# Two attention blocks on one core: phi's weight folded into theta's, z as keys, small jobs through one PSUM bank, loops unrolled

## The reference

```python
# block 1 (no softmax), 64 inner channels
g_x, theta_x, phi_x = W_g x + b_g, W_theta x + b_theta, W_phi x + b_phi
y = ((theta_x.T @ phi_x) / 1024) @ g_x.T
x = x + W_out y.T + b_out
# block 2, 128 channels; z is block 1's result
theta, phi = W_t z + b_t, W_p z + b_p
attn = softmax(theta.T @ phi / sqrt(128))
out = z + W_c (z attn.T) + b_c
```

## Time and profile before

| what | us |
|---|---|
| median of 3 runs | 178.74 |
| lowest, highest | 178.66, 178.77 |
| span of the profiled execution, first to last instruction | 176.7 |
| TensorE busy | 170.2 (96%) |
| VectorE busy | 131.4 (74%) |
| ScalarE busy | 103.1 (58%) |
| GpSimd busy | 35.8 (20%) |

### The profile page before, as it was taken

One profiled execution on the slowest core, in us unless ns is written; L12 is line 12 of the kernel. 1 busy time (PEld: TensorE's weight loads), 2 busy tenths in 40 slices (PEclk: granted clock), 3 DMA queues, 4 the chain that ended last, 5 costly groups with the idle time before them and its releaser, 6 DMA issues.

```text
span 176.7 us, 2720 instructions
## 1 busy us (share of the span) xinstructions
PE 170.2 (96%) x974; PEld 138.9 (79%) x974; DVE 131.4 (74%) x189; ACT 103.1 (58%) x176; POOL 35.8 (20%) x32
## 2 busy tenths in 40 slices
PE   7899998999999999999999999999999999998994
PEld 7784585788889887888889787988888888876794
DVE  0315889886987776896988676796989689899811
ACT  3024477858683365958684274958686557656410
POOL 1105600003102200543202200443302202340000
PEclk9999999999999999999999999999999999999999
DMA  4600000003001000013001000010000100100011
GB/s 137 190 0 0 4 0 0 0 4 118 1 2 59 2 4 0 0 59 91 32 0 57 3 0 0 0 59 0 0 0 18 41 4 0 59 2 0 0 63 59
DMA packets 2537, 4.71 MB, mean 27 GB/s; under 512 B 288, under 2 KB 992, under 8 KB 2528
## 3 DMA queue, kind: packets, MB, share of 16 engines
q1 hardware_dynamic: 2096, 4.26, 7.1%
q10 hardware_dynamic: 432, 0.33, 0.8%
HBM read 2.49 MB, written 2.10 MB: 26 GB/s over the span
## 4 chain that ended last, share of the span: by engine, by line
PE 83%; DVE 5%; ACT 5%; DMA 4%; SPq 1%; issue 1%; ACTq 0%; DVEq 0%
PE ring L254 29%; PE ring L334 21%; PE turned L304 14%; PE ring L262 4%; DMA X<-x_dram 4%; ACT P L567 3%; PE ring L244 3%; PE ring L317 3%; PE ring L208 2%; DVE negmax L695 2%; DVE PT_lo L710 2%; ACT PT_hi L576 2%; PE ring L219 2%; PE turned L208 1%; PE ring L495 1%; PE ring L288 1%
## 5 line engine op out<-in xcount | busy, mean ns | idle before, releaser
L576 ACT ACTIVATE PT_hi<-turned 128x512 fp32r<-128x512 f32 x62 | 35.9, 595 | 26.5 <-PE turned L304 26.5
L695 DVE TENSOR_REDUCE negmax<-ring 128x1 f32<-128x1024 f32 x32 | 39.1, 1222 | 15.3 <-PE ring L254 15.1
L567 ACT ACTIVATE P<-ring,negmax 128x1024 f32<-128x1024 f32 x32 | 35.8, 1118 | 19.0 <-DVE negmax L695 19.0
L710 DVE TENSOR_TENSOR PT_lo<-turned,PT_hi 128x512 fp32r<-128x512 f32 x62 | 42.1, 684 | 5.2 <-ACT PT_hi L576 4.7
L304 PE MATMUL turned<-identity,P 128*128 128x128 f32 x256 | 36.1, 274 | 2.1 <-DVE P L703 1.6
L304 PEld LDWEIGHTS turned<-identity,P 128*128 128x128 f32 x256 | 30.4, 141 | 9.0 <-DVE P L703 1.6
L703 DVE TENSOR_SCALAR P<-P,rden 128x1024 f32<-128x1024 f32 x32 | 27.0, 845 | 1.1
L334 PE MATMUL ring<-PT_hi,V_hi 128*128 128x512 f32 x56 | 23.5, 420 | 0.1
L334 PE MATMUL ring<-PT_lo,V_hi 128*128 128x512 f32 x56 | 22.2, 396 | 0.0
L334 PE MATMUL ring<-PT_hi,V_lo 128*128 128x512 f32 x56 | 22.1, 395 | 0.0
L254 PE MATMUL ring<-Phi_hi,T_hi 128*128 128x512 f32 x62 | 21.3, 424 | 0.0
(11 more groups left out here) (101 smaller groups left out, 200.3 us busy)
## 6 DMA issues: line engine op xcount, KB each, us to landing
out_dram<-result SPq DMA_DIRECT2D x7, 256.0 KB, 2.0
X<-x_dram SPq DMA_DIRECT2D x3, 512.0 KB, 3.3
X_first<-x_dram SPq DMA_DIRECT2D x2, 256.0 KB, 4.1
w<-weights_dram ACTq DMA_DIRECT2D x1, 194.0 KB, 5.8
out_dram<-result SPq DMA_DIRECT2D x1, 192.0 KB, 1.9
wi<-inner_dram SPq DMA_DIRECT2D x1, 64.2 KB, 5.9
pg_w<-pg_weights_dram ACTq DMA_DIRECT2D x1, 64.0 KB, 3.2
pg_b<-pg_bias_dram ACTq DMA_DIRECT2D x1, 64.0 KB, 5.5
```

Of the source, the lines that this page charges most:

```text
L567: nc.scalar.activation(P[:, t % P_BUFFERS, :], ring[:, slots[t], :], ACT.Exp, bias=negmax[:, t:t + 1], accum_out=den[:, t:t + 1]).then_inc ...
L576: nc.scalar.activation(PT_hi[:, g, half_chunks(h), k * TILE:(k + 1) * TILE], turned[:, columns(h)].rearrange("p (j r) -> p j r", j=CHUNKS_ ...
L695: nc.vector.tensor_reduce(negmax[:, t:t + 1], ring[:, slots[t], :], AX.X, ALU.max, negate=True).then_inc(max_ready, 1)
L710: nc.vector.tensor_tensor(PT_lo[:, g, half_chunks(h), rows], turned[:, columns(h)].rearrange("p (j r) -> p j r", j=CHUNKS_PER_HALF), PT_hi ...
```

## The change

What it does:

- **Scores from z.** `theta.T phi` is `(W_t z + b_t).T (W_p z + b_p)`. Once, at the start, U is made from both weights (two transposes, one 128-column product, three one-column products, scaled by 128^-0.5 in ScalarE's copy). Per image only `t = U z + u` is computed, and the keys are z itself, in its high and low part. The phi conv and its evacuation are gone. What phi's bias adds to a query's row of scores is constant over the row; it is carried as `rho`, two extra columns of the values' weight (`VW`, 130 columns), and added to the row's maximum: after `row_max` a new operation on 128x1, `shift`, waits for the maximum and gives the bias of the exp.
- **Padding.** M, R and the inner weights, 64 rows before, are 128 rows with zeros.
- **One bank for small jobs.** PSUM is now `ring` (two slots of two banks, scores only), `turned`, `numer` and one bank `aux`. All jobs for image b+1 go through `aux`, in the order pg0, pg1, MT, R, A, Z0, Z1, t0, V0, V1, V2, t1. Each waits until the one before has been evacuated (`aux_free`). pg, z and t are made in halves, the values in three parts.
- **Order.** No hardware loops. One sequence of 32 tiles, n = 0 to 31; in tile n: scores(n+2), half a turn, `job_one`, a piece of attend (from n = 4), half a turn, `job_two`. The values of image b+1 are made in image b.
- **First image.** x, z and t of image 0 go by three passes too; V in three parts between, with their evacuations.
- **Engines.** High parts of x and z of the later images are made by GpSimd instead of ScalarE. The residual operation is gone: the last bias is added in `copy_numer`, and `finish` adds z. x has two buffers, z three, t and V two.

The core of the diff, in the order of the new file:

```diff
-        w = sb("w", [C, W_COLS])
-        wi = sb("wi", [CI, I_COLS])
+        wi = sb("wi", [C, I_COLS])
+        w = sb("w", [C, 2 * C])
+        bias = sb("bias", [C, 4])
+        VW = sb("VW", [C, V_COLS])
+        U = sb("U", [C, C + 3])
+        UT_hi, UT_lo = sb("UT_hi", [C, C], F32R), sb("UT_lo", [C, C], F32R)
...
-        ring = ctx.enter_context(nc.psum_tensor("ring", [C, 3, PIX], F32))
-        numer, small = ring[:, 2, 0:BANK], ring[:, 2, BANK:PIX]
+        ring = ctx.enter_context(nc.psum_tensor("ring", [C, 2, PIX], F32))
+        numer = ctx.enter_context(nc.psum_tensor("numer", [C, BANK], F32))
+        aux = ctx.enter_context(nc.psum_tensor("aux", [C, BANK], F32))
...
+            def job_pg(b, half):
+                pe.wait_ge(aux_free, aux_before(b, f"pg{half}"))
+                if half == 0:
+                    pe.wait_ge(x_loaded[b], 16)
+                phi_g_chunks(b, aux, half).then_inc(aux_ready, 1)
...
+            def queries(b, bank, cols):
+                return three(bank, (UT_hi[:, :], UT_lo[:, :]), (Z_hi[:, b % 2, :], Z_lo[:, b % 2, :]), cols)
+            def job_t(b, half):
+                pe.wait_ge(aux_free, aux_before(b, f"t{half}"))
+                if b:
+                    pe.wait_ge(z_lo, (b - 1) * HALVES + half + 1)
+                queries(b, aux[:, :], columns(half)).then_inc(aux_ready, 1)
...
+            job_A(0)
+            pe.wait_ge(aux_free, aux_after(0, "A"))
+            for half in range(HALVES):
+                pe.wait_ge(first_x_lo, half + 1)
+                affine_half(ring[:, 1, columns(half)], half).then_inc(first_z, 1)
+            pe.wait_ge(u_lo, 1)
+            pe.wait_ge(first_z_lo, 1)
+            queries(0, first_t_bank(0), FIRST_T[0]).then_inc(first_t, 1)
+            pe.wait_ge(first_z_ready, 1)
...
+            value_chunks(0, numer, 0).then_inc(first_v, 1)
+            scores(0)
+            queries(0, first_t_bank(1), FIRST_T[1]).then_inc(first_t, 1)
+            job_t(0, 1)
+            pe.wait_ge(first_z_ready, 2)
+            scores(1)
+            for part in (1, 2):
+                pe.wait_ge(first_v_lo, part)
+                value_chunks(0, numer, part).then_inc(first_v, 1)
...
+            for n in range(ALL - 1):
+                b, t = divmod(n, TILES)
+                if n + 2 < ALL:
+                    scores(n + 2)
+                turn(n, 0)
+                if b + 1 < IMAGES:
+                    job_one(b + 1, t)
+                if n >= GT:
+                    attend(n // GT - 1, n % GT)
+                turn(n, 1)
+                if b + 1 < IMAGES:
+                    job_two(b + 1, t)
+            attend(ALL_GROUPS - 2, PIECES - 1)
...
+            first_z_copy(0)
+            act.wait_ge(u_copied, 1)
+            first_t_high(0)
+            first_z_copy(1)
+            first_v_high(0)
+            first_t_high(1)
+            high_t(0, 1)
+            exps(0)
+            exps(1)
+            first_v_high(1)
+            first_v_high(2)
...
+            for n in range(ALL - 1):
+                b, t = divmod(n, TILES)
+                high_turned(n, 0)
+                if b + 1 < IMAGES:
+                    job_one(b + 1, t)
+                if n + 2 < ALL:
+                    exps(n + 2)
+                high_turned(n, 1)
+                if n >= GT and n % GT == GT - 1:
+                    copy_numer(n // GT - 1)
+                if b + 1 < IMAGES:
+                    job_two(b + 1, t)
...
+                dve.wait_ge(max_ready, n + 1)
+                nc.vector.tensor_scalar(shift[:, t:t + 1], negmax[:, t:t + 1], rho[:, b % 2, t:t + 1],
+                                        rho[:, b % 2, t:t + 1], ALU.subtract, ALU.add).then_inc(shift_ready, 1)
...
+            first_z_low(0)
+            first_t_low(0)
+            first_z_low(1)
+            first_v_low(0)
+            first_t_low(1)
+            row_max(0)
+            low_t(0, 1)
+            row_max(1)
+            norm(0)
+            first_v_low(1)
+            first_v_low(2)
...
+            for n in range(ALL - 1):
+                b, t = divmod(n, TILES)
+                if n + 2 < ALL:
+                    row_max(n + 2)
+                low_turned(n, 0)
+                if b + 1 < IMAGES:
+                    job_one(b + 1, t)
+                norm(n + 1)
+                low_turned(n, 1)
+                if b + 1 < IMAGES:
+                    job_two(b + 1, t)
...
+            def split_z(b, half):
+                count = (b - 1) * HALVES + half + 1
+                cols = columns(half)
+                pool.wait_ge(aux_free, aux_after(b, f"Z{half}"))
+                nc.gpsimd.tensor_copy(Z_hi[:, b % 2, cols], Z[:, b % Z_BUFFERS, cols]).then_inc(z_hi, 1)
+                pool.wait_ge(z_hi, count)
+                nc.gpsimd.tensor_tensor(Z_lo[:, b % 2, cols], Z[:, b % Z_BUFFERS, cols],
+                                        Z_hi[:, b % 2, cols].bitcast(F32), ALU.subtract).then_inc(z_lo, 1)
```

More of the change, by code:

```diff
@@ L339, in _ @@
             pe.wait_ge(idle_ready, 1)
             for _ in range(WARM_UP):
-                nc.tensor.matmul(small[:, 0:C], idle[:, :], idle[:, :], start=True, stop=True)
+                nc.tensor.matmul(aux[:, 0:C], idle[:, :], idle[:, :], start=True, stop=True)
             pe.wait_ge(pg_w_loaded, 16)
-            for h in range(HALVES):
-                pe.wait_ge(first_loaded[h], 16)
-                phi_g_chunks(ring[:, PG_SLOT, :], X_first,
-                             half_range(h)).then_inc(half["pg"] if h == 0 else pg_ready, 1)
```

1026 lines of the change are left out of this document (472 added, 554 removed).

## The result

The changed kernel takes 187.37 us (median; 187.16 to 188.59), the kernel before 178.75 on the same chip: a ratio of 1.050, 95% interval 1.047 to 1.053. The profiled execution of the changed kernel spans 185.6 us against 176.7, 8.9 more where the forecast had 2.8 more.

What follows compares the result with a forecast made beforehand. TensorE was taken as the bound, with an equally tight ring through VectorE and ScalarE. Tile 8 at 63.6, two images 78.6, last tiles to 169.9 and 9.6 after gave span 179.5; plus 2.04, 181.5 us, range 178.4 to 184.4.

Steps and rivals of the forecast that it cites:

- The shift: Between maximum and exp: 0.20 us a tile (0.15 to 0.35), free in job tiles, about 1 us in all.
- norms beside GpSimd: On VectorE: a norm beside a GpSimd operation takes 1.16 us against 0.75; more of these, hidden in job tiles.
- middle images of about 39 us: Images 1 and 2, scores(8) to scores(16): 39.3 us each, 1.0 less than the 40.3 replaced.
- The opening: Start to tile 0: added waits; z's first half at 14.2, scores(0) from 17.2, loop start at 26.95 us.
- the stand: TensorE before tile 0: idle 22.95 to 26.45, 3.5 us, waiting for the low part of V part 1.
- The waits of pg1, Z0, t0 and V0 in the first image: TensorE's jobs in the first image wait for evacuations: 1.25, 1.0, 0.65 and 0.45 us.
- rival (c): After the 3.5 us of idleness before tile 0 the clock falls to half rate: 2.2 us, 183.7; chance 0.10.
- the ring: Dependent steps through VectorE and ScalarE, each tile: period 3.66 us, as tight as TensorE's, growing to 3.86.
- Phi's removal: Images 1 to 3 lose six 512-column passes, 1.47 us each, 4.4 us of TensorE time where it never rests.
- the 0.5 of job changes or the 0.3 of padding alone: TensorE, per image: five or six more job changes add 0.5 us; padding adds nothing, -0.3 its good bound.
- Jobs in these images find their bank emptied: Middle images: evacuation just fits the 1.8 us between jobs; only V0 is 0.2 late once.
- Rival (b): VectorE becomes the bound: shift 0.35 or more and norms at 1.16 make the ring 4.2; 185.0 us, chance 0.14.

Runs made afterwards that it cites:

- experiment 5: Changed kernel with 54 idle matmuls filling TensorE's stand between parts 1 and 2 of the first image's values: 186.31 us, ratio 1.042.
- experiment 1: Changed kernel without the 32 shift operations, the exp taking the negated maximum itself: 181.69 us, ratio 1.018 to the kernel before.
- Experiment 4: Kernel before, with a dependent 128x1 operation added between each row maximum and its exp: 182.43 us, ratio 1.024.
- experiment 2: Changed kernel with GpSimd's X_lo and V_last each made in four operations of 256 columns: 187.55 us, ratio 1.051 to the kernel before.
- experiment 10: Changed kernel with t's passes of images 1 to 3 done twice, repeating what phi's removal took away: 190.50 us, ratio 1.067.
- experiment 8: Changed kernel without rho, values in two parts, X_lo and V_last in pieces, pg1 and t0 of image 1 in numer, 28 idle matmuls: 173.07 us, ratio 0.969.
- experiments 8 and 9: Experiment 8 at 173.07 us, and the same kernel without its 28 idle matmuls at 173.09 us, ratio 0.967.
- experiment 3: Changed kernel with part 2 of the first image's values moved behind the first half turn of tile 0: 184.36 us, ratio 1.031.

## Why the prediction was right, and where it was wrong

Forecast was 181.5 us, 178.4 to 184.4; measured 187.37. The direction was right, the size was not. Two steps failed. The shift was priced at 0.20 a tile, free in tiles with jobs and about 1 us in all; it adds 0.37 and costs 7.6. And norms beside GpSimd were priced at 1.16 and hidden; three took 1.96 to 2.38 and cost 2.3 us. The clock's 1.1 was a rival left out of the sum. Two of the forecast's own signs failed with these steps: middle images of about 39 us (40.57 and 40.73) and maxima 3.8 to 3.9 apart (4.02).

**The opening: right, by its steps.** z, t and the scores came 0.9 us sooner than worked out (16.27 against 17.2), the stand was 3.63 where 3.5 was said and began 0.8 sooner, the first maximum came 1.0 sooner (19.66), and tile 0 started 0.26 from the forecast. The chain that made it (VectorE's first maximum, low_t, second maximum, ScalarE's exps, V's high copy, its low part) is the one that was written down. The waits of pg1, Z0, t0 and V0 in the first image are within some 0.3 of theirs; V1's 0.15 did not come. At a clock of 1.00 tile 8 starts at 63.28 (experiment 5) against 63.6. That closeness is partly luck, for two misses cancel in it: the shift lies on this chain too and costs 2.0 up to tile 8 (experiment 1), more than was counted; the rest was counted too high.

**The clock: rival (c), left out of the forecast.** It had 0.10 and 2.2 us; it came, and cost 1.1. The row that it leaned on, the first eight pg passes, doesn't carry it: the granted clock reads 1.00 from 4 to 6 us, where these took 2.07, and the same passes took 1.51 in the changed kernel, at 1.00 too. What made them long stays open. The reason that held was the other one: the forecast had itself put 3.5 us of idleness ahead of tile 0, so the rival deserved more than 0.10. The Trainium skill (TensorE: Matmul & The Clock Gate, Part 1: The HAM clock gate) says that an idle array falls back to half rate, and the granted clock of 0.50 behind the stand agrees.

**The shift: the term that was most wrong.** "None is in the trace; the nearest is the reciprocal, 0.153 us, with 0.04 to its follower. I take 0.20; ends 0.15 and 0.35." Two faults are in this step. First its size: a record of 0.27, and 0.37 from start to start, just beyond the far end. The reciprocal's row is that of an operation whose operand lies ready, while the shift waits for the maximum to end and the exp waits for the shift; a link in a chain is to be priced from one operation's start to the next one's. Second, its reach: "Where jobs stretch a tile to 5 us it is free." In tiles 8 and 16 it isn't (0.7 in tile 8), because lag brought from the job-less tiles ahead of them is paid for there, in a copy that a job waits for. In the last image, where 1 us was counted, it costs 2.7. And the kernel before had the answer in its rows: two periods of 3.66 side by side mean that an addition to the ring has no room in a tile without jobs. Experiment 4 shows it there: 0.3 more from maximum to maximum, 3.6 us over the kernel.

**The norms beside GpSimd: a row read for the wrong thing.** "A norm beside a GpSimd operation took 1.16 ... more of these, hidden in job tiles." The overlap behind that row was 0.63 us long; the norm ended about half a microsecond after the GpSimd operation in every case (0.53 to 0.55), so its length is set by when it starts. The three that start early take 1.96 to 2.38, and experiment 2 gets 2.3 us for them, 0.8 of it in each of images 1 and 3's stretch and 0.65 in image 2's. The Trainium skill (GPSIMD Engine Reference, 8. Key points) says that GpSimd shares its SBUF interfaces with VectorE, with contention for VectorE instructions in a two-port mode or with two inputs in SBUF. The rows agree in that it is the norm, whose 1024 elements come from SBUF, that is stretched, while an operation with an input in PSUM keeps its 0.68 inside GpSimd's operation, and the 128x1 reciprocal its 0.15. GpSimd first, then VectorE:

```profile
149.35 2.44 POOL L829 TENSOR_TENSOR V_last<-V_hi,V_lo 128x1024 f32<-128x1024 f32 x1
```

```profile
149.59 0.68 DVE L684 TENSOR_TENSOR PT_lo<-turned,PT_hi 128x512 fp32r<-128x512 f32 x1
150.19 0.15 DVE L675 RECIPROCAL rden<-den 128x1 f32<-128x1 f32 x1
150.38 1.96 DVE L677 TENSOR_SCALAR P<-P,rden 128x1024 f32<-128x1024 f32 x1
```

No run here shows which mode the norm is in.

**Phi's removal: right in work, too high in worth.** Six passes an image went, as counted. But "these lie in the stages where TensorE never rests" was true of the kernel before only. In the changed kernel, where the ring has grown to 4.02, they are worth 2.6 (experiment 10).

**Middle images.** Without the shift, image 1 takes 39.27 (experiment 1), which looks like the forecast and is a coincidence: it has a stretched norm of some 0.75 in it. Without both it takes 38.55 (experiment 8), 0.75 under the forecast. That is more than the 0.5 of job changes or the 0.3 of padding alone could give back, and experiment 8 has V in two parts besides; the runs don't part these. "Jobs in these images find their bank emptied" was wrong in two places, by 0.37 (pg1, the shift) and 0.54 (M, the norm). No run tests padding, the unrolled loops or the moved residual alone; what can be said is that with all of them in place the kernel without shift, rho and long GpSimd operations takes 173.1 (experiments 8 and 9).

**The sum.** 6.1 us more span than forecast: 0.8 before tile 8 (the clock's 1.1, less 0.3), 2.7 in the images (shift 2.8 and norms 1.5, less 1.5 for the images' better base), 2.6 behind them (shift 2.7 against 1.0 counted, norm 0.85). The causes overlap in part, so this is a tally of separate removals and not a strict sum. The forecast's direction held, its range (to 184.4) didn't: the bound on the shift reached 1.2 us up where the truth was 6.6 above the term. Rival (b) came nearest, VectorE as the bound by a shift of 0.35 or more and norms slowed by GpSimd, priced at 185.0 with 0.14. Its kind of cause is the one that the runs show, but not its places: it put 3.5 us into some ten tiles with V and t, and these give 0.2 and 0.3 for an image (tiles 12 and 13, experiment 5 against 1), while tiles 8 and 16 and the last image have more; and it took the norms at 1.16. That 185.0 and the clock's 1.1 make 186.1 is therefore in part luck. It had too little weight because its first condition was the far end of a price that had been guessed from the wrong kind of row.

**One correction to what stands ahead of the prediction.** It says there that rho is added to the row's maximum. The new operation subtracts rho and adds it back, so it moves only the rounding of the exp's bias. The time of the operation doesn't hang on that, but its worth does: the operation that cost most changes nothing but rounding.

## What to carry to other kernels

Compare the period of each ring of dependent steps with the bottleneck engine's period before adding anything to it: where they were equal here, 32 operations of 128x1 and 0.27 us each cost 3.6 us, and 7.6 in the changed kernel, where work taken off TensorE came back only in part. Price a new link from start to start of operations that wait for one another, never from the record of one whose operand lay ready. When work moves to GpSimd, look at what VectorE runs beside it; a row that shows a short overlap says nothing of a long one, and cutting the GpSimd operation into pieces removed most of the cost although GpSimd took 0.9 us longer.

## What the runs showed of the hardware that was not expected

- VectorE's norm (fp32, 128x1024, SBUF to SBUF, 0.75 us alone) beside GpSimd's two-input operation of 1024 columns (2.37) ends some 0.55 us after that one's end, wherever inside that operation the norm began: 1.16, 1.96, 2.38, and without the shift, where it began 0.19 behind the GpSimd operation, 2.73. Beside operations of 256 columns it took 0.75 to 1.36. A norm that had begun first (46.01, the GpSimd operation of 512 columns at 46.26) kept its 0.75, and the GpSimd operation took 1.66 instead of 1.28.
- After a stand of 3.63 us the granted clock fell to 0.50 for about 2 us, and cost 1.1 us. Behind the stand of 2.99 us in experiment 1's profiled execution it kept 1.00. It fell ahead of the stand too, in some executions of one and the same kernel (from 12 to 20 us in one of experiment 3's five; the other four have a mean of 1.00). So it isn't settled by the kernel's idle times alone, as far as these can be seen; more the runs don't show.
- GpSimd's copy to fp32r took 1.04 us for 1024 columns and 0.61 for 512, less than half of its two-input subtraction (2.37); the forecast had bounded it by 0.5 and 1.3.
